# Weighing four units of attention at once in every second slot, with six buffers of exponentials

## The chip, the cores and the metric

The kernel runs on one core of a Trainium2 chip. A core has a matrix engine (TensorE; PE in the profile, its weight loads PEld), a vector engine (VectorE, DVE), an activation engine (ScalarE, ACT), GpSimd (POOL) and SyncE (SP), which issues most transfers. Each engine runs its own list of instructions in order; semaphores hold them together. The metric is the device time of one execution in microseconds (us). The kernel before takes 1525.11 us, the median of three runs (1524.86 to 1526.01).

## The reference, cut to what matters

The input is a batch of eight images of 32 x 32 positions (1024 tokens) with 256 channels, in float32. Three layers follow each other, each added to its input:

```python
x = x + conv_ref(gn(x), ...)   # linear attention: 8 heads of 32; out = q @ (k^T v) / n
t = to_tokens(x)               # 8 batches x 1024 tokens x 256
t = t + attn_ref(ln(t), ...)   # softmax attention:
#   scores = q @ k^T / sqrt(32);  attn = softmax(scores);  sa = attn @ v;  out = sa @ w_agg + b_agg
t = t + ffn_ref(ln(t), ...)    # 8 experts: gates by 8 Sinkhorn iterations, each expert takes its
#   128 best tokens per batch, multiplies them by its 256 x 256 matrix and puts them back
```

The softmax attention is the largest part: per batch and head 1024 x 1024 scores, their exponentials, and the product of the exponentials with the values.

## The kernel before, in words

**Units, slots, steps.** The softmax attention of one batch is 64 units (2 groups of four heads, 4 blocks of 256 queries, 8 tiles of 128 keys). A unit has three parts. `scores(u)`, on the matrix engine (L918), is four matmuls, one for each head, over the full width of 128 columns, into one of two PSUM tiles `score_ps[u % 2]`. `exponential(u)`, on the activation engine (L1209), is one instruction of 128x1024 elements into `probs[:, u % PROBS, :]`. `weigh(u)`, on the matrix engine again (L940), multiplies the exponentials by the values: each head needs only 32 columns, so four matmuls stand in the four column quarters of the array (`tile_position=(0, 32 r)`) and run beside each other. Float32 matmuls are two instructions each, so that a unit is four L918 instructions and eight L940 ones in the trace. The row sums of the exponentials are added up by the vector engine for the first six key tiles of a block (`add_up`, L1607) and by the matrix engine for the last two (L937), in the same narrow form; `total` (L950) ends a block of eight units.

Two units make a slot, so a batch has 32 slots and the eight batches 256. Beside the units the slots carry steps: the linear attention and the projections of the next batch (its "front": `xT`, `gmean`, `gvar`, `xn`, `qk0`, `v0`, `qT`, `dots`, `lin`, `zT`, `proj`, `v`, `norms`) and the end of the batch before (its "store": `agg`, `z2T`, `gate`). In batches 5 to 7 (counted from 0) the routing of the experts is merged in. `order()` lists the steps with entries `("rest", n)`, which leave n slots free of them; `spread()` deals the list to slots by the weights in `WORK`, and `Slot.halves` cuts each slot's steps in two.

**The order inside a slot k** is, on the matrix engine:

```python
for u in (2 * k + 2, 2 * k + 3): scores(u)
for st in first: step(*st)
weigh(2 * k)
weigh(2 * k + 1)
for st in second: step(*st)
```

and on the activation engine `exponential(2k+2)`, first half of the steps, `exponential(2k+3)`, second half.

**What waits for what.** `scores(u)` waits for `exponential(u - 2)`, which frees its PSUM tile. `exponential(u)` waits for `scores(u)`, and for `weigh(u - PROBS)` and for the vector engine's sum of unit `u - PROBS`, which free its buffer. `weigh(u)` waits for `exponential(u)`; `total` waits for the last sum of its block. The steps of the matrix engine share three PSUM banks in turn (`shared_ps`); each is filled by a step, read by ACT or DVE, and can then be filled again. Some steps also need a result at once: `proj` (L962) needs the copies `chan` that ACT makes (L1137) of the transposes `zT` (L957); `gmean` (L962 on `small`) needs the statistics that DVE makes of `xT`; `xn` on DVE (L1417) needs a reciprocal root that POOL works out in 14 small instructions (L361 to L366) after `gvar`.

**The tail.** Experts' tokens are gathered and put back by `indirect_dma_start` on POOL (`pick`, L1309, and `put`, L1319), in batch 7 and behind it. The descriptors of these transfers are written by POOL into a scratch region of the on-chip memory, whose size is an argument of the program's constructor.

## Time and profile before

| | us |
|---|---|
| median of three runs | 1525.11 |
| the profiled execution's own time | 1524.4 |
| its span in the profile | 1520.8 |
| matrix engine busy | 1343.5 (88%) |
| vector engine busy | 1017.4 (67%) |
| activation engine busy | 864.4 (57%) |
| GpSimd busy | 549.0 (36%) |

The time outside the span is 3.6 us. In the trace the attention of batch 0 runs from 110 to 267 us, batches 1 to 4 take 153 us each up to 880, batch 5 goes to 1040, batch 6 to 1206, batch 7 to about 1370, and the rest is the tail. A matmul's start in a row is recorded and its end is modelled, so the text works with differences of starts. In a row, `x16` says how many instructions were merged, and the brackets at its end give the idle time before it and what ended it.

### The profile page before, as it was taken

The numbers are of one execution on the slowest core, as the hardware profiler recorded it, in microseconds if no ns is written. First come the engines' busy times: TensorE is split into PE (matmuls) and PEld (weight loads), VectorE is DVE, ScalarE is ACT, GpSimd is POOL, SyncE is SP. The second block draws the span as 40 slices with busy tenths as digits, with TensorE's granted clock in tenths as the row PEclk, the third lists the DMA queues.
The fourth block names the chain that finished last, engine by engine and source line by source line (L and its number), as shares of the span: only waits on it lengthen the run. The fifth ranks groups of instructions, "written<-read, shape, count | busy, mean of one in ns | idle before, by whom it ended". The sixth has DMA issues, their size and how long they took to land.

```text
span 1520.8 us, 29096 instructions
## 1 busy us (share of the span) xinstructions
PE 1343.5 (88%) x10849; PEld 917.5 (60%) x10849; DVE 1017.4 (67%) x2077; ACT 864.4 (57%) x1260; POOL 549.0 (36%) x1126
## 2 busy tenths in 40 slices
PE   4688989999999999999999999899998988887633
PEld 3555566667666766676667666657665656555522
DVE  3416766758575857585758575977789757588781
ACT  1346657667666766676667666566656664342100
POOL 1341620345034503450345034412353046643443
PEclk7999999999999999999999999999999998997666
DMA  2043003600360036003600360027000573433422
GB/s 76 3 127 81 2 29 84 167 15 29 84 167 15 29 84 167 15 29 84 167 15 29 84 167 15 1 72 195 27 1 1 133 216 104 119 118 105 123 73 81
DMA packets 66787, 119.15 MB, mean 78 GB/s; under 512 B 10705, under 2 KB 46546, under 8 KB 66642
## 3 DMA queue, kind: packets, MB, share of 16 engines
q1 hardware_dynamic: 56640, 90.47, 22.1%
q0 software_dynamic: 8960, 26.75, 5.9%
q8 instruction: 89, 1.46, 0.4%
q14 instruction: 56, 0.46, 0.1%
q10 hardware_dynamic: 1042, 0.01, 0.0%
HBM read 29.11 MB, written 33.55 MB: 41 GB/s over the span
## 4 chain that ended last, share of the span: by engine, by line
PE 57%; DVE 24%; issue 7%; ACT 4%; POOL 4%; another core or an unknown queue 2%; DMA 0%; POOLq 0%; DVEq 0%; ACTq 0%
PE shared L962 27%; PE scores L918 11%; PE acc L940 10%; DVE prob_sum L1607 6%; PE acc L937 4%; DVE acc_sb L1581 3%; ACT probs L1209 3%; PE shared L957 2%; DVE bn L1340 2%; PE acc L950 2%; DVE best_i L1513 1%; DVE work L1515 1%; DVE best L1511 1%; DVE bn_x L1393 1%
## 5 line engine op out<-in xcount | busy, mean ns | idle before, releaser
L1209 ACT ACTIVATE probs<-scores 128x1024 f32<-128x1024 f32 x512 | 516.7, 1023 | 180.7 <-PE scores L918 91.7
L918 PE MATMUL scores<-query_stack,key_stack 96*128 96x256 f32 x2048 | 343.3, 308 | 13.9 <-ACT probs L1209 11.3
L1607 DVE TENSOR_TENSOR prob_sum<-prob_sum,probs 128x512 f32<-128x512 f32 x512 | 333.0, 712 | 0.0
L918 PEld LDWEIGHTS scores<-query_stack,key_stack 96*128 96x128 f32 x2048 | 275.3, 190 | 83.8 <-issue 42.3
L940 PE MATMUL acc<-probs,v_all 128*32 128x256 f32 x4096 | 293.2, 390 | 7.0 <-issue 5.3
L1242 POOL TENSOR_TENSOR attn_T<-acc_sb 128x256 f32<-128x256 f32 x56 | 45.7, 817 | 447.0 <-DVE acc_sb L1581 442.9
L962 PE MATMUL shared<-w_sb,chan 128*128 128x512 f32 (+1 forms) x512 | 188.0, 503 | 5.0 <-DVE chan L1417 5.0
L940 PEld LDWEIGHTS acc<-probs,v_all 128*32 128x32 f32 x4096 | 115.8, 110 | 107.3 <-issue 42.4
L962 PEld LDWEIGHTS shared<-w_sb,chan 128*128 128x128 f32 x512 | 92.1, 193 | 67.8 <-issue 63.7
L962 PE MATMUL shared<-chan,w1T 128*128 128x512 f32 x256 | 120.9, 606 | 1.6 <-ACT chan L1137 1.6
L1581 DVE RECIPROCAL acc_sb<-acc_sb 128x256 f32<-128x256 f32 x64 | 111.4, 1741 | 0.0
L1466 DVE TENSOR_TENSOR lo<-shared,hi 128x512 fp32r<-128x512 f32 x64 | 43.4, 684 | 99.6 <-ACT hi L1162 99.6
L1607 DVE TENSOR_TENSOR prob_sum<-probs 128x512 f32<-128x512 f32 x128 | 98.8, 812 | 11.4 <-PE acc L950 8.9
L1432 DVE TENSOR_REDUCE ss<-v_all 128x16 f32<-128x512 f32 x64 | 43.8, 684 | 91.0 <-ACT v_all L1151 90.9
L1144 ACT ACTIVATE lo<-shared 128x512 f32<-128x512 f32 x64 | 38.2, 597 | 107.6 <-PE shared L962 107.6
L937 PE MATMUL acc<-probs,ones 128*32 128x256 f32 x1024 | 84.8, 395 | 1.4 <-issue 1.1
L962 PEld LDWEIGHTS shared<-chan,w1T 128*128 128x128 f32 x256 | 46.7, 192 | 49.8 <-issue 49.2
L1192 ACT ACTIVATE hi<-shared 128x512 f32<-128x512 f32 (+1 forms) x31 | 16.0, 515 | 102.7 <-PE shared L1079 54.2
L1471 DVE TENSOR_REDUCE norm_max<-shared 128x1 f32<-128x512 f32 x64 | 43.6, 682 | 41.3 <-PE shared L962 41.3
L1162 ACT ACTIVATE hi<-shared 128x512 fp32r<-128x512 f32 x64 | 37.5, 594 | 49.4 <-PE shared L962 49.4
L957 PE MATMUL shared<-ident,rows 128*128 128x128 f32 x252 | 43.6, 286 | 22.2 <-ACT rows L1116 14.2
L962 PE MATMUL shared<-waggT,attn_T 128*128 128x256 f32 x244 | 61.4, 387 | 1.7 <-ACT hi L1192 1.7
(216 smaller groups left out, 2069.0 us busy)
## 6 DMA issues: line engine op xcount, KB each, us to landing
query_stack<-hi SPq DMA_DIRECT2D x120, 128.0 KB, 2.5
key_stack<-hi SPq DMA_DIRECT2D x120, 128.0 KB, 2.5
x_sb<-in_x_dram SPq DMA_DIRECT2D x8, 1024.0 KB, 5.3
out_dram<-resid SPq DMA_DIRECT2D x16, 512.0 KB
tokens_scratch<-resid SPq DMA_DIRECT2D x16, 512.0 KB
tokens_scratch<-rows SPq DMA_DIRECT2D x16, 512.0 KB, 4.7
key_stack<-lo SPq DMA_DIRECT2D x60, 128.0 KB, 2.5
query_stack<-lo SPq DMA_DIRECT2D x60, 128.0 KB, 2.5
```

Of the source, the lines that this page charges most:

```text
L918: last = pe.matmul(score_ps[u % 2][:, QB * r:QB * (r + 1)], key_stack[stack, HG * g + r, P * kt:P * (kt + 1)], query_stack[stack, HG * g + ...
L937: pe.matmul(acc[DH * r:DH * (r + 1), QB:2 * QB], ones[:, 0:DH], p[:, QB * r:QB * (r + 1)], start=False, stop=False, skip_group_check=True, ...
L940: last = pe.matmul(acc[DH * r:DH * (r + 1), 0:QB], v_all[:, g, kt, DH * r:DH * (r + 1)], p[:, QB * r:QB * (r + 1)], start=kt == 0, stop=kt ...
L957: last = pe.transpose(ps[:, P * j:P * (j + 1)], m, ident[:, :])
L962: last = pe.matmul(out, stationary, moving, start=j == 0, stop=j == len(pairs) - 1)
L1209: act.activation(probs[:, u % PROBS, :], score_ps[u % 2][:, :], ACT.Exp, scale=DH ** -0.5) \
L1242: pool.tensor_tensor(attn_T[:, g, QB * qb:QB * (qb + 1)], acc_sb[:, 0:QB], acc_sb[:, QB:2 * QB], ALU.mult).then_inc(s["attn_ready"], 1)
L1432: dve.tensor_reduce(ss[:, t, :], squares[:, t % 2, :].rearrange("p (h d) -> p h d", d=DH), AX.X, ALU.add).then_inc(s["squares_summed"], 1)
L1466: read(dve.tensor_tensor(lo[:, j, part].bitcast(F32R), ps[:, :], hi[:, j, part], ALU.subtract), seg, *st)
L1471: read(dve.tensor_reduce(norm_max[:, seg.front, j, h:h + 1], ps[:, :], AX.X, ALU.max), seg, *st)
L1581: dve.reciprocal(acc_sb[:, QB:2 * QB], acc_sb[:, QB:2 * QB]).then_inc(s["recip_ready"], 1)
L1607: dve.tensor_tensor(total[:, part], probs[:, (u - 1) % PROBS, part] if kt == 1 else total[:, part], probs[:, u % PROBS, part], ALU.add).th ...
```

## The change

Three constants and the list of steps change. In slots with an odd number the matrix engine now weighs four units in a row, in slots with an even number none; `scores` and `exponential` stay where they were, two in each slot.
```diff
-PROBS = 4
+PROBS = 6
@@ order()
-    steps = [("rest", 0.5), ("xT", 1, 0), ("xT", 0, 1), ("agg", 0), ("agg", 1), ("agg", 2), ("agg", 3),
+    steps = [("xT", 1, 0), ("rest", 0.5), ("xT", 0, 1), ("agg", 0), ("agg", 1), ("agg", 2), ("agg", 3),
...
@@ the matrix engine's loop over slots
-                if k is not None:
-                    weigh(2 * k)
-                    weigh(2 * k + 1)
+                if k is not None and k % 2:
+                    for u in range(2 * k - 2, 2 * k + 2):
+                        weigh(u)
                     if k % BLOCK_PAIRS == BLOCK_PAIRS - 1:
                         total(k // BLOCK_PAIRS)
@@ kernel()
-    nc = _bacc.Bacc("TRN2", target_bir_lowering=False, num_devices=1)
+    nc = _bacc.Bacc("TRN2", target_bir_lowering=False, num_devices=1,
+                     dynamic_dma_scratch_size=8192)
```

Three places show how it moves instructions. In the order of a program a float32 matmul counts once, so a unit is x4 of `acc<-probs,v_all`.

The first is the matrix engine in slots 20 to 23 of batch 1, where few steps lie. Before:

```order
L918 MATMUL scores<-query_stack,key_stack 128x256 x8
L940 MATMUL acc<-probs,v_all 32x256 x8
L918 MATMUL scores<-query_stack,key_stack 128x256 x8
L940 MATMUL acc<-probs,v_all 32x256 x8
L918 MATMUL scores<-query_stack,key_stack 128x256 x8
L962 MATMUL shared<-hi 128x128 x8
L940 MATMUL acc<-probs,v_all 32x256 x8
L918 MATMUL scores<-query_stack,key_stack 128x256 x8
```

Now:

```order
L918 MATMUL scores<-query_stack,key_stack 128x256 x16
L957 MATMUL shared<-ident,lo 128x128 x4
L940 MATMUL acc<-probs,v_all 32x256 x16
L918 MATMUL scores<-query_stack,key_stack 128x256 x8
L962 MATMUL shared<-hi 128x128 x6
L918 MATMUL scores<-query_stack,key_stack 128x256 x8
L962 MATMUL shared<-hi 128x128 x2
```

The scores of slots 20 and 21 (x16) stand next to each other with nothing between them, and one group of four units follows where two groups of two were; the transposes `ident,lo` (step `qT`) came from slot 19, and one of the `lin` steps (`hi`) went to slot 23.

The second is the vector engine in slots 1 to 4 of batch 0: `small` are the statistics of the steps `x_stats`, `gmean` and `gvar` (L1412), `chan` is `xn`, `prob_sum` the sums of the units. Before:

```order
L1400 COPY small<-mv_x 128x2
L1403 COPY small<-shared 128x2
L1406 TENSOR_TENSOR small<-small 128x2
L1407 TENSOR_TENSOR small<-small 128x2
L1408 TENSOR_TENSOR small<-small,mv_x 128x2
L1607 TENSOR_TENSOR prob_sum<-prob_sum,probs 128x512 x4
L1471 TENSOR_REDUCE norm_max<-shared 128x1
L1412 TENSOR_SCALAR small<-shared 128x2
L1417 TENSOR_SCALAR chan<-chan,small 128x512 x2
L1607 TENSOR_TENSOR prob_sum<-prob_sum,probs 128x512 x4
```

Now:

```order
L1400 COPY small<-mv_x 128x2
L1607 TENSOR_TENSOR prob_sum<-prob_sum,probs 128x512 x4
L1471 TENSOR_REDUCE norm_max<-shared 128x1
L1403 COPY small<-shared 128x2
L1406 TENSOR_TENSOR small<-small 128x2
L1407 TENSOR_TENSOR small<-small 128x2
L1408 TENSOR_TENSOR small<-small,mv_x 128x2
L1412 TENSOR_SCALAR small<-shared 128x2
L1607 TENSOR_TENSOR prob_sum<-prob_sum,probs 128x512 x4
L1417 TENSOR_SCALAR chan<-chan,small 128x512 x2
```

The last sums of the first block (the second x4) stood behind `chan` and now stand ahead of it; the product `gmean` is read one slot later.

The third is the matrix engine in slots 24 and 25 of batch 1. Before:

```order
L957 MATMUL shared<-ident,rows 128x128 x8
L940 MATMUL acc<-probs,v_all 32x256 x8
L962 MATMUL shared<-chan,w1T 128x512 x4
L918 MATMUL scores<-query_stack,key_stack 128x256 x8
L962 MATMUL shared<-chan,w1T 128x512 x2
```

Now:

```order
L957 MATMUL shared<-ident,rows 128x128 x8
L962 MATMUL shared<-chan,w1T 128x512 x4
L918 MATMUL scores<-query_stack,key_stack 128x256 x8
L962 MATMUL shared<-chan,w1T 128x512 x2
L962 MATMUL shared<-norm_sq,head_ones 128x512
```

The group of narrow matmuls that stood between the transposes `zT` (L957) and the first `proj` (`chan,w1T`) is gone from there.

## Rows read from the trace of the kernel before

**Rows 1.** The page: busy us, share of the span and instructions of each engine.

```profile
PE 1343.5 (88%) x10849; PEld 917.5 (60%) x10849; DVE 1017.4 (67%) x2077; ACT 864.4 (57%) x1260; POOL 549.0 (36%) x1126
```

**Rows 2.** Windows, batches 3, 5, 6: length, busy PE, PEld, DVE, ACT, POOL; clock; DMA.

```profile
573.85:727.00 153.15, 151.03 (x1309) 102.87 (x1306) 103.90 (x194) 105.63 (x154) 52.66 (x125) 1.00 0.28 74
...
880.00:1040.20 160.20, 153.57 (x1297) 102.42 (x1296) 124.05 (x243) 103.25 (x150) 52.69 (x125) 1.00 0.26 69
1040.20:1206.20 166.00, 155.60 (x1310) 105.42 (x1306) 133.34 (x281) 105.72 (x153) 58.81 (x125) 0.98 0.23 61
```

**Rows 3.** Timeline, batch 2, slots 20 to 22: start, duration, engine, instructions.

```profile
517.12 1.21 PE L918 MATMUL scores<-query_stack,key_stack 96*128 96x256 f32 x8
518.26 1.07 PE L940 MATMUL acc<-probs,v_all 128*32 128x256 f32 x16
519.26 1.36 PE L918 MATMUL scores<-query_stack,key_stack 96*128 96x256 f32 x8
...
521.56 1.21 PE L918 MATMUL scores<-query_stack,key_stack 96*128 96x256 f32 x8
...
522.33 1.94 ACT L1209 ACTIVATE probs<-scores 128x1024 f32<-128x1024 f32 x2 [0.35 <-PE scores L918]
522.61 1.95 PE L962 MATMUL shared<-hi 128*128 128x128 f32 x16
```

**Rows 4.** Timeline in windows of 0.15 us: single matmuls about slot 23, batch 2.

```profile
525.16 0.40 PE L940 MATMUL acc<-probs,v_all 128*32 128x256 f32 x4
525.49 0.39 PE L918 MATMUL scores<-query_stack,key_stack 96*128 96x256 f32 x1
...
525.71 0.52 PE L918 MATMUL scores<-query_stack,key_stack 96*128 96x256 f32 x3
526.31 0.40 PE L918 MATMUL scores<-query_stack,key_stack 96*128 96x256 f32 x2
526.64 0.42 PE L937 MATMUL acc<-probs,ones 128*32 128x256 f32 x4
```

**Rows 5.** Timeline, batch 2, slot 19: one long group of narrow matmuls.

```profile
515.28 0.61 PE L940 MATMUL acc<-probs,v_all 128*32 128x256 f32 x8
515.72 0.61 PE L937 MATMUL acc<-probs,ones 128*32 128x256 f32 x8
```

**Rows 6.** Lines, 410 to 570 us: ACT's steps, mean ns of one.

```profile
L1116 ACT ACTIVATE rows<-resid,ln_b,ln_r 128x256 f32<-128x256 f32 x8 | 4.6, 592 | 2.5 <-POOLq L1256 2.5
L1157 ACT ACTIVATE hi<-shared,gb 128x512 f32<-128x512 f32 x4 | 3.1, 772 | 0.0
L1132 ACT ACTIVATE hi<-shared 128x256 f32<-128x256 f32 x8 | 3.0, 389 | 0.0
```

**Rows 7.** Timeline, batch 2, slots 14, 15, 24: what ACT gives to the matrix engine.

```profile
494.92 1.03 ACT L1209 ACTIVATE probs<-scores 128x1024 f32<-128x1024 f32 x1 [1.08 <-DVE prob_sum L1607]
...
497.64 0.74 PE L918 MATMUL scores<-query_stack,key_stack 96*128 96x256 f32 x4 [0.50 <-ACT probs L1209]
...
530.78 1.10 ACT L1137 ACTIVATE chan<-shared 128x512 f32<-128x512 f32 x2
531.11 1.07 PE L940 MATMUL acc<-probs,v_all 128*32 128x256 f32 x16
```

**Rows 8.** Timeline, batch 3, slot 2: the wait of `gmean`.

```profile
586.09 1.03 PE L962 MATMUL shared<-waggT,attn_T 128*128 128x256 f32 x4
588.42 0.35 PE L962 MATMUL shared<-small,gn_mean 128*128 128x2 f32 x2 [1.29 <-DVE small L1400]
```

**Rows 9.** Timeline, batch 0, slots 2 and 3: DVE and PE.

```profile
124.75 1.00 DVE L1417 TENSOR_SCALAR chan<-chan,small 128x512 f32<-128x512 f32 x2 [3.67 <-POOLq L1268]
...
128.22 0.64 PE L950 MATMUL acc<-prob_sum,ones 128*32 128x256 f32 x8 [3.67 <-DVE prob_sum L1607]
```

**Rows 10.** Timeline of POOL, batch 7: the last gathers of a burst of nine.

```profile
1253.86 0.94 POOL L1309 DMA_INDIRECT hi<-tokens_scratch,slot_token  x1 [0.30 <-issue]
1255.11 0.94 POOL L1309 DMA_INDIRECT hi<-tokens_scratch,slot_token  x1 [0.30 <-issue]
```

More of the change, by code:

```diff
@@ new lines, in order @@
+             ("store_rows", 0), ("rest", 1), ("store_rows", 1), ("gmean",), ("agg", 7), ("store_rows", 2),
+             ("gvar",), ("store_stats", 1), ("xn", 0), ("z2T", 0), ("store_rows", 3), ("z2T", 1), ("z2T", 2),
+             ("z2T", 3), ("gate", 0), ("rest", 2), ("qk0", 0), ("gate", 1), ("store_rows", 4), ("qk0", 1),
+             ("gate", 2), ("store_rows", 5), ("xn", 1), ("store_rows", 6), ("z2T", 4), ("rest", 1), ("gate", 3),
[3 rows of a table added]
+             ("head_scale", 0), ("resid", 3), ("resid", 4), ("v0", 6), ("head_scale", 1), ("qk0", 7), ("resid", 5),
@@ L109, in order @@
+             ("zT", 1, 0), ("rest", 0.25), ("zT", 0, 0), ("proj", 0, 0), ("front_rows", 4), ("square", 0, 0),
+             ("proj", 2, 0), ("proj", 1, 0), ("norms", 0, 0), ("square", 1, 0), ("front_rows", 5),
+             ("front_rows", 6), ("front_rows", 7), ("norms", 1, 0), ("square", 2, 0), ("proj", 3, 0), ("zT", 0, 1),
              ("zT", 1, 1), ("norms", 2, 0), ("proj", 0, 1), ("square", 3, 0), ("proj", 1, 1), ("rest", 0.5),
```

21 lines of the change are left out of this document (5 added, 16 removed), and 3 rows, old and new, of the table steps.

## The prediction

> **What bounds the kernel now.** I read the page's engine shares, then windows of one batch each, then the timeline of one steady batch, then single matmuls. The matrix engine is busy 88% of the span and the others 67% or less [rows 1]. In batch 3, which stands for batches 1 to 4, it is busy 151.0 of 153.2 us at clock 1.00, with DVE at 104 and ACT at 106 [rows 2]: there the matrix engine sets the time. In batches 5 and 6 DVE has 124 and 133 us of work, and the batches take 160 and 166: there the sinkhorn and top-k steps on DVE hold the matrix engine back in the middle of the batch. Batch 7 and the tail hang partly on the gathers.
>
> **What a group of narrow matmuls costs beyond its matmuls.** Inside a long group a unit takes 0.44 us [rows 5], two quartets of 0.22. Around a group [rows 4]: the last quartet starts at 525.16 and the first scores at 525.49, 0.33 and not 0.22; the second scores follow at 525.71, 0.22 later, where the next five take 0.12 each (525.71 to 526.31); and the last two steps, 526.31 to 526.64, are 0.33, of which 0.12 is one cadence and 0.21 the way into the next group. So a group costs 0.11 + 0.10 + 0.09 = 0.30; its first quartet is some 0.02 longer. The group of two units alone agrees (518.26 to 519.26 [rows 3]): 1.00 where two units inside a long group are 0.87. The 0.10 may be less behind transposes; without it the price is 0.22. I take 0.31.
>
> The Trainium skill (TensorEngine Tiling, section Tiling Modes, Key Properties) says that changing the tiling mode drains the engine and gives no price. By it the merged group would save the same, so the sum doesn't change.
>
> **Term 1, fewer groups.** Eight batches of 32 slots are 256 groups; 128 remain. 128 x 0.31 = 40 us, or 5.0 us per batch (28 to 41 us over all by the two ends). In the middle of batches 5 and 6 and in the second half of batch 7, about 20 of the 128, the matrix engine waits for others anyway, so some 6 of the 40 don't show.
>
> **Term 2, the cover that goes.** The weighing also hid the exponentials. From the start of a slot's scores to the first exponential 0.77 us pass (521.56 to 522.33), and two exponentials take 1.94 [rows 3], so the second ends 2.71 us into the slot. The second scores of the next slot need it. In an even slot with steps of length c the matrix engine gets there after 1.05 (two scores, 521.56 to 522.61) + c + 0.47. The wait is therefore 1.25 - c (with some 0.05 for the signal), plus the time A of those steps that ACT does between its two exponentials. Before, 1.09 us of weighing and its entry stood in between, and the rule gives 0.16 for an empty slot; the row shows 0.15 (scores of 1.36 at 519.26 against 1.21 at 517.12 [rows 3]), so I trust it. With ACT's steps of 0.59, 0.77 and 0.39 [rows 6], the even slots of a steady batch in the new order are:
>
> - slots 16, 20 and 30 have no step on the matrix engine: 3 x 1.25 = 3.75;
> - slot 14 has two `qT` transposes (c 0.88, A 0.77): 1.14;
> - slot 4 has c 1.28 (three or four `z2T`, a `gate`), and ACT does z2T, store_rows, z2T between the exponentials, A 1.37: 1.34;
> - slot 2 has one `agg` (c 0.86): 0.4; slots 0, 6 to 12, 18, 22 to 28 have 1.3 or more of c against it: 0.
>
> That is 6.6. In slots 24 and 26 another cover goes: `proj` needs the copies of `zT`, which ACT finished at 530.78 + 1.10 = 531.88, while the group that began at 531.11 hid it [rows 7]. Without the group `proj` starts 0.8 late, twice: 1.6. Term 2 is 8.2 us per steady batch. In an odd slot four units take at least 1.74 + 0.31 us, so nothing waits there.
>
> **Term 3, waits that go.** `gmean` waits 1.46 us in every steady batch (586.09 to 588.42, less the 0.86 of `agg` [rows 8]). It moves behind the next slot's scores, and its statistics are then ready. In slot 15 the scores wait because the exponential before them waited 1.08 for DVE's sum to free its buffer [rows 7]; six buffers lift that wait, about 0.8. Five waits of 0.16 as above are replaced by term 2's: 0.8. Together 3.1. The `dots` and `norms` waits, 0.6 together, I leave.
>
> **The other batches.** *Batches 1 to 4:* -5.0 + 8.2 - 3.1 = +0.1 each, that is 0. *Batch 0:* `gmean` waits for its statistics and `total` waits for the last sums, which stand behind `xn`, which waits 3.67 for POOL [rows 9]. Now those sums stand ahead of `xn`, and `gmean` is a slot later. 3.7 goes there, `gmean`'s wait (taken as the 1.46 of [rows 8]) and 5.0 of groups go too, and new waits of about 1 in slot 2 and 3 in slots 24 to 30 come: -6.2. What comes in the middle falls beside older waits. *Batch 5:* -4 for groups, -2.7 for old waits as in a steady batch, +4 for even slots (sinkhorn products fill some, DVE's waits swallow others): -2.7. *Batch 6:* -3.5, -1.5, +3.5: -1.5. *Batch 7:* in slots 2 to 10 new waits of 3.5 against some 2.5 of old ones for DVE's sums of the kind in [rows 7] (an estimate), groups -3 where they show: -2. *The tail and the front:* same instructions, 0.
>
> **Buffers and scratch.** The two buffers cost no instruction. The gathers follow each other at 1.25 us in a burst of nine with 0.30 between them [rows 10]: POOL isn't short of descriptor space there, and I take 0 for half the scratch. The bounds are 0 and one landing time per burst, of which I have no row; by the nearest rows, one step of 1.25 us for each of the eight bursts or so, 10 us.
>
> The Trainium skill (SBUF - State Buffer, section SBUF size: 192, 224, or 256?) gives 16 KiB per partition to the ring of descriptors that GpSimd fills. By it the change leaves 8 KiB, and this is the one rule that speaks against it. No row here shows a ring that is full.
>
> **Sum.** 4 x 0 - 6.2 - 2.7 - 1.5 - 2 = -12.4, with the 0.1 left over per steady batch -12, say -13 us since the 0.6 of `dots` and `norms` can only shrink. The profiled execution took 1524.4 us (span 1520.8 and 3.6 around it), 0.7 under the median, so 1511 us. In totals: the groups give 35, old waits give some 26, new waits take some 48. The result is a small difference of large terms, and this sets the range.
>
> **The clock.** New waits are at most 1.3 us each. Batches 1 to 4 keep 1.00 with waits of 1.46 in them, batch 5 too, and batch 6 shows 0.98 [rows 2]. I take no loss; a batch at 0.98 would cost 3 us. The Trainium skill (TensorE: Matmul & The Clock Gate, Why this matters for your kernels) warns of idle gaps between bursts of matmuls; by the rows the new ones are too short for it, and the sum stays.
>
> **Rivals.**
>
> *A, the cover isn't needed (15%).* Half of the new waits don't appear, because ACT runs ahead with six buffers or because dependent steps were late anyway: 1511 - 24 = 1487. For it: in batches 5 to 7 others' waits can swallow them. Against it: `scores(u)` needs `exponential(u - 2)` whatever the number of `probs` buffers, and the check on an empty slot above was exact.
>
> *B, slower: steps without the pause (14%).* Before, every slot had 1 us in which ACT and DVE emptied the three shared banks and made operands. In the 10 even slots with steps, that pause is gone. If each of them loses 0.4 us on banks and operands beyond what I have counted, 7 batches x 10 x 0.4 = 28 us: 1539. It decides from 0.19 us per such slot, where it eats my 13 us. For it: the copies of `zT` show one such case at 0.8. Against it: ACT and DVE have 48 us free per batch, and a bank is refilled only after two other steps.
>
> *C, the scratch stalls POOL (3%).* 10 us, all in batch 7 and the tail: 1521.
>
> *D, nothing comes of it (12%).* New waits are 13 us larger than I count, for instance since ACT's steps push both exponentials in more slots: 1524.
>
> **How the numbers follow.** My forecast has 56%. Its own range is 1500 to 1520, from 0.22 to 0.32 per group (12 us) and from 20% on either side of 48 us. The range reaches from rival A's time to just over D's, 1488 to 1528. Within 0.2% (3 us, about what a measurement of this kernel tells from none) is D and a little of B, C and the forecast: 0.13. Faster: A's 15, C's 2, nearly all of the forecast's 56 and the space between: 0.73. Slower: 0.14.
>
> **What the new profile would show.** Groups of four units 1.87 us long; scores in slots 17, 21, 31 with a wait of 1.2 on ACT `probs`, slot 15 with 1.1; steady batches of 153 us again, batch 0 near 150; `gmean` without a wait; `total` of batch 0's first block without its 3.67; ACT's waits for `prob_sum` nearly gone; POOL's gathers still 1.25 us apart in bursts. I am wrong if steady batches are under 150 (term 2 too large) or over 156 (rival B, seen as waits for `chan`, `hi` or DVE results in even slots).

## The result, and the profile after

The changed kernel takes 1531.76 us (median of 5 runs, 1530.11 to 1532.86) where the kernel before takes 1525.11: ratio 1.0042, 95% interval 1.0028 to 1.0057. It is 0.4% slower. I had forecast 1511 us, in a range of 1488 to 1528, and gave slower a chance of 0.14. The prediction was wrong.

The page of the kernel after: engine shares, then four groups of instructions (busy us, mean ns | idle us before them, releaser).

```profile
PE 1321.5 (87%) x10849; PEld 933.2 (61%) x10849; DVE 1016.9 (67%) x2077; ACT 860.4 (56%) x1260; POOL 560.2 (37%) x1126
...
L1209 ACT ACTIVATE probs<-scores 128x1024 f32<-128x1024 f32 x512 | 511.9, 1024 | 121.5 <-PE scores L918 102.8
L918 PE MATMUL scores<-query_stack,key_stack 96*128 96x256 f32 x2048 | 344.8, 308 | 34.6 <-ACT probs L1209 32.4
...
L1607 DVE TENSOR_TENSOR prob_sum<-prob_sum,probs 128x512 f32<-128x512 f32 x512 | 332.8, 710 | 0.0
...
L962 PE MATMUL shared<-chan,w1T 128*128 128x512 f32 x256 | 122.4, 612 | 10.1 <-ACT chan L1137 8.7
```

The instruction counts are those of [rows 1], and the matrix engine is busy 22 us less: half of the groups, and the pauses around them, are gone. But the scores now wait 34.6 us, 32.4 of it for ACT's exponentials, and `proj` waits 8.7 us for ACT's copies. DVE's sums wait for nothing. The same two lines on the page of the kernel before:

```profile
L918 PE MATMUL scores<-query_stack,key_stack 96*128 96x256 f32 x2048 | 343.3, 308 | 13.9 <-ACT probs L1209 11.3
L962 PE MATMUL shared<-chan,w1T 128*128 128x512 f32 x256 | 120.9, 606 | 1.6 <-ACT chan L1137 1.6
```

Windows of the kernel after, in the columns of [rows 2]: batch 0, then 3, 5, 6, then 7.

```profile
110.20:271.00 160.80, 143.17 (x1224) 96.24 (x1224) 105.75 (x169) 102.67 (x144) 45.17 (x92) 0.96 0.21 50
...
574.70:726.50 151.80, 145.99 (x1300) 103.06 (x1296) 103.80 (x194) 104.58 (x152) 54.00 (x125) 1.00 0.28 74
878.40:1041.50 163.10, 153.04 (x1316) 107.45 (x1312) 122.94 (x243) 104.82 (x152) 52.83 (x125) 0.99 0.26 69
1041.50:1208.50 167.00, 153.07 (x1310) 107.47 (x1306) 132.50 (x281) 105.14 (x153) 63.27 (x125) 0.97 0.23 61
...
1208.60:1376.80 168.20, 141.49 (x1197) 102.80 (x1193) 109.51 (x245) 79.26 (x109) 82.38 (x105) 0.92 0.45 136
```

The window of batch 3 in [rows 2] reaches 1.1 us into batch 4. Cut to the batch, the kernel before shows:

```profile
573.85:725.91 152.06, 149.94 (x1300) 101.78 (x1296) 103.90 (x194) 104.73 (x152) 52.66 (x125) 1.00 0.28 74
```

In batch 3 the matrix engine is busy some 4 us less than before and idle 3.7 us more, and the batch is nearly as long. What the groups gave went into waits.

A batch is measured here from the start of its first own scores to the next batch's (batch 7's to the start of its slot 30). In us (the differences are of unrounded times, the last column is the sum of my terms in the prediction):

| batch | before | after | difference | forecast |
|---|---|---|---|---|
| 0 | 159.4 | 160.9 | +1.5 | -6.2 |
| 1 | 152.7 | 151.8 | -0.8 | 0 |
| 2 to 4, each | 152.1 | 151.8 | -0.2 | 0 |
| 5 | 162.3 | 163.1 | +0.8 | -2.7 |
| 6 | 166.0 | 167.0 | +1.0 | -1.5 |
| 7 | 160.2 | 168.2 | +8.0 | -2 |
| from there to the end | 154.4 | 149.3 | -5.0 | 0 |

The steady batches came out as forecast in all, and several pairs of slots did by themselves: 30-31 are 0.86 longer (worked out: 1.25 less 0.16 less 0.31 is 0.78), 2-3 are 1.19 shorter (0.4 - 1.46 - 0.31 is -1.37), 24-25 are 0.59 longer (0.8 - 0.31 is 0.49), and four pairs with enough work are 0.31 to 0.34 shorter (0-1, 12-13, 22-23, 28-29). In the other pairs the moved steps mix with the grouping (8-9 are 1.4 shorter, 20-21 are 1.3 longer). The new waits stand where they were expected. Timelines of the kernel after, batch 3: the scores of slot 21 behind an empty slot 20, and `proj` behind `zT` in slot 24.

```profile
667.85 1.22 PE L918 MATMUL scores<-query_stack,key_stack 96*128 96x256 f32 x8
...
668.63 2.88 ACT L1209 ACTIVATE probs<-scores 128x1024 f32<-128x1024 f32 x3
669.70 0.74 PE L918 MATMUL scores<-query_stack,key_stack 96*128 96x256 f32 x4 [0.64 <-ACT probs L1209]
670.62 0.74 PE L918 MATMUL scores<-query_stack,key_stack 96*128 96x256 f32 x4 [0.17 <-ACT probs L1209]
```

```profile
682.34 1.08 ACT L1137 ACTIVATE chan<-shared 128x512 f32<-128x512 f32 x2
683.52 3.67 PE L962 MATMUL shared<-chan,w1T 128*128 128x512 f32 x8 [0.79 <-ACT chan L1137]
```

Eight matmuls of scores take 1.21 us without a wait [rows 3]. Here the two units of slot 21 start 1.85 and 2.77 us behind the start of slot 20. ACT goes from one exponential to the next, and the matrix engine is bound to it.

The old waits went too. Timeline of the kernel after, batch 3, slots 2 and 3: `gmean` waited 1.29 in [rows 8] and waits 0.18.

```profile
588.37 0.74 PE L918 MATMUL scores<-query_stack,key_stack 96*128 96x256 f32 x4 [0.18 <-ACT probs L1209]
589.29 0.35 PE L962 MATMUL shared<-small,gn_mean 128*128 128x2 f32 x2 [0.18 <-DVE small L1400]
```

The miss lies in batches 0, 5, 6 and 7, by 7.7, 3.5, 2.5 and 10 us; the tail gives 5.0 of it back, for which I had no term. The tail's gain is no gain of the grouping: it takes 149.6 us in `e3` below too, which is the kernel before but for the scratch. And batch 6 is not a firm number: the changed kernel's takes 163.9 to 167.0 us from one trace to another. One place in batch 0 stands out. Its slots 22 and 23 took 12.0 us and take 18.0. Timeline and windows of the kernel after, about slot 22 of batch 0.

```profile
216.15 1.08 PE L957 MATMUL shared<-ident,rows 128*128 128x128 f32 x4 [3.15 <-ACT rows L1116]
216.88 2.06 PE L918 MATMUL scores<-query_stack,key_stack 96*128 96x256 f32 x8
218.74 1.06 PE L957 MATMUL shared<-ident,rows 128*128 128x128 f32 x4
220.53 3.75 PE L962 MATMUL shared<-chan,w1T 128*128 128x512 f32 x4 [0.73 <-issue]
224.21 1.65 PE L940 MATMUL acc<-probs,v_all 128*32 128x256 f32 x16
```

```profile
216.00:220.00 4.00, 3.65 (x16) 3.27 (x16) 2.64 (x8) 1.80 (x4) 2.99 (x9) 0.50 0.82 262
220.00:224.50 4.50, 3.97 (x8) 1.38 (x12) 0.00 (x0) 0.61 (x2) 1.52 (x8) 0.50 0.00 0
```

`zT` waits 3.15 us for ACT's rows, and the matmuls behind it run at a granted clock of 0.50, the lower level of 1.2 GHz: scores of 2.06 where 1.21 is usual, `proj` of 3.75 where it takes about 2. The stretch lasts 10 us.

The kernel before had lost its clock in batch 0 too, three times for 3.4 us, and once behind waits far shorter than these. Timeline and window of the kernel before, batch 0, slots 18 and 19:

```profile
203.04 0.74 PE L918 MATMUL scores<-query_stack,key_stack 96*128 96x256 f32 x4 [1.06 <-ACT probs L1209]
204.62 1.22 PE L918 MATMUL scores<-query_stack,key_stack 96*128 96x256 f32 x4 [0.84 <-ACT probs L1209]
```

```profile
204.00:208.00 4.00, 3.38 (x28) 2.03 (x32) 2.18 (x8) 2.50 (x3) 1.22 (x6) 0.57 0.00 0
```

### The profile page after: what moved, and what is told of

It is laid out like the page before. It is cut to its first block, busy times and chain, and to the rows that moved or that the text cites. A ratio compares the mean times of both kernels' runs of the same rounds, so it can differ in the third digit from the quotient of the medians.

```text
span 1526.0 us, 29094 instructions
## 1 busy us (share of the span) xinstructions
PE 1321.5 (87%) x10849; PEld 933.2 (61%) x10849; DVE 1016.9 (67%) x2077; ACT 860.4 (56%) x1260; POOL 560.2 (37%) x1126
## 3 DMA queue, kind: packets, MB, share of 16 engines
q8 instruction: 89, 1.46, 0.4%
## 4 chain that ended last, share of the span: by engine, by line
PE 57%; DVE 19%; issue 9%; ACT 7%; POOL 6%; another core or an unknown queue 1%; ACTq 0%; POOLq 0%; DVEq 0%
PE shared L962 29%; PE acc L940 10%; PE scores L918 10%; DVE prob_sum L1607 5%; ACT probs L1209 3%; PE acc L937 3%; PE shared L957 2%; PE acc L950 2%; DVE acc_sb L1581 1%; DVE best_i L1513 1%; DVE work L1515 1%; DVE best L1511 1%; DVE bn L1340 1%; ACT chan L1137 1%
## 5 line engine op out<-in xcount | busy, mean ns | idle before, releaser
L1209 ACT ACTIVATE probs<-scores 128x1024 f32<-128x1024 f32 x512 | 511.9, 1024 | 121.5 <-PE scores L918 102.8
L918 PE MATMUL scores<-query_stack,key_stack 96*128 96x256 f32 x2048 | 344.8, 308 | 34.6 <-ACT probs L1209 32.4
L940 PE MATMUL acc<-probs,v_all 128*32 128x256 f32 x4096 | 279.0, 388 | 1.8 <-issue 1.7
L962 PE MATMUL shared<-w_sb,chan 128*128 128x512 f32 (+1 forms) x512 | 184.9, 499 | 6.1 <-DVE chan L1417 5.8
L940 PEld LDWEIGHTS acc<-probs,v_all 128*32 128x32 f32 x4096 | 122.1, 111 | 101.9 <-issue 30.9
L1607 DVE TENSOR_TENSOR prob_sum<-probs 128x512 f32<-128x512 f32 x128 | 92.1, 760 | 0.0
L1199 ACT ACTIVATE acc_sb<-acc 128x512 f32<-128x512 f32 x64 | 38.0, 593 | 66.3 <-PE acc L950 53.9
L1253 POOL TENSOR_SCALAR ln_v<-mv 128x4 f32<-128x4 f32 x30 | 11.0, 367 | 155.6 <-DVE mv L1358 154.2
```

The source lines that it names most:

```text
L918: last = pe.matmul(score_ps[u % 2][:, QB * r:QB * (r + 1)], key_stack[stack, HG * g + r, P * kt:P * (kt + 1)], query_stack[stack, HG * g + ...
L940: last = pe.matmul(acc[DH * r:DH * (r + 1), 0:QB], v_all[:, g, kt, DH * r:DH * (r + 1)], p[:, QB * r:QB * (r + 1)], start=kt == 0, stop=kt ...
L962: last = pe.matmul(out, stationary, moving, start=j == 0, stop=j == len(pairs) - 1)
L1209: act.activation(probs[:, u % PROBS, :], score_ps[u % 2][:, :], ACT.Exp, scale=DH ** -0.5) \
L1607: dve.tensor_tensor(total[:, part], probs[:, (u - 1) % PROBS, part] if kt == 1 else total[:, part], probs[:, u % PROBS, part], ALU.add).th ...
```

## The experiments

The ratios are to the kernel before on the same chip, with their 95% intervals. The kernel before itself took 1521.4, 1500.1, 1521.6, 1499.4 and 1521.5 us in the five comparisons: there are two kinds of chip here. Times are compared within a comparison, and pieces of a trace across comparisons only for batches 0 to 6. These show no difference between the kinds, but one trace differs from another of the same kernel by up to 0.8 us in batch 0, 2 us in batches 3 and 4 and 3 us in batch 6.

### Taking the change apart

`e1_old_steps` keeps the grouping, the buffers and the scratch, and takes the list of steps back.

```diff
-    steps = [("xT", 1, 0), ("rest", 0.5), ("xT", 0, 1), ...
+    steps = [("rest", 0.5), ("xT", 1, 0), ("xT", 0, 1), ...   # as before, whole list
```

> The change with the list of steps of the kernel before: four units weighed in every odd slot, six buffers, half the scratch, steps as they were. Theory G (grouping saves 0.31 us a group and takes the cover from even slots; the loss against forecast is in batch 0 slots 22-23, where the new list puts a transpose that waits for ACT rows and the clock halves, and in batch 7): batch 0 gets back some 5 of its 6 us there, steady batches lose the moved gmean (1.5 us each) and get more waits in slots 2 and 4: 1530 to 1540 in all. Rival S (the new steps are to blame): under 1520.

Measured: 1563.33 us, ratio 1.0281 (1.0250 to 1.0311), 23 us over the range expected. Slots 22 and 23 of batch 0 came down to 10.7 us without a half clock, as expected. But batches 1 to 4 take 157.5 to 160.8 us and batches 5 and 6 169.0 and 169.8, and in each of batches 2 to 4 the granted clock is at 0.50 for 3.4 to 6.8 us: on the old list the grouping costs far more in a steady batch than the moved `gmean`.

`e2_pairs_new_steps` keeps all but the grouping.

```diff
-                if k is not None and k % 2:
-                    for u in range(2 * k - 2, 2 * k + 2):
-                        weigh(u)
+                if k is not None:
+                    weigh(2 * k)
+                    weigh(2 * k + 1)
```

> The change without the grouping: two units weighed in every slot as before, with the new list of steps, six buffers and half the scratch. Theory G: the groups cost again 0.31 us each but the cover is back; gmean's wait (1.46 us, batches 1 to 6), DVE's sums (0.8) and batch 0's 3.7 us are gone: 1505 to 1515, batch 7 near 160 us. Rival S (new steps) or rival R (half the scratch): 1530 or more. If six buffers and the new list bring nothing: 1525.

Measured: 1512.32 us, ratio 0.9946 (0.9927 to 0.9965). Batches 154.5, four times 151.8, 161.9, 166.4, 156.6.

`e3_scratch` is the kernel before with the smaller scratch alone.

```diff
-    nc = _bacc.Bacc("TRN2", target_bir_lowering=False, num_devices=1)
+    nc = _bacc.Bacc("TRN2", target_bir_lowering=False, num_devices=1,
+                     dynamic_dma_scratch_size=8192)
```

> The kernel before with half the scratch for dynamic DMAs and nothing else. Theory G: no difference, 1525 within 1. Rival R (half the scratch stalls POOL's gathers and puts in batch 7 and the tail): 1530 to 1535, batch 7 near 168 us instead of 160.

Measured: 1522.63 us, ratio 1.0003 (0.9988 to 1.0018).

`e4_six_buffers` adds the two buffers to it.

```diff
-PROBS = 4
+PROBS = 6
```

> The kernel before with six buffers of exponentials and half the scratch, pairs weighed in every slot, old steps. Theory G: the exponentials no longer wait for DVE's sums: slot 15 wins 0.8 us in batches 1 to 6, a bit more in the DVE-bound middles of 5 and 6 and in batch 7: 1515 to 1521. Rival R: 1530.

Measured: 1514.54 us, ratio 0.9960 (0.9946 to 0.9975); batch 0 is 5.4 us shorter than before, batch 7 2.0. In batch 0 slots 18-19 give 3.0 of it (the kernel before has a half clock there, this one not), 22-23 1.8 and 30-31 0.5; slots 0 to 5 are as long as before.

What follows: half the scratch costs nothing. Six buffers give 0.4%, mostly in batch 0. The new list with two units per slot adds little (0.9946 against 0.9960, intervals that overlap). The grouping then loses: from 0.9960 to 1.0281 on the old list, from 0.9946 to about 1.004 on the new one. The list was needed for the grouping, and even with it the grouping costs 0.9% (`e9` and `e10` below).

### Is the price of a group real?

`e7_split_groups` starts from the two-unit kernel and splits the group in eight slots of batches 1 to 6.

```diff
+                split = k is not None and 32 <= k < 224 and k % 32 in (1, 8, 9, 10, 11, 12, 28, 29)
+                if split:
+                    weigh(2 * k)
                 for st in first:
                     step(*st)
                 if k is not None:
-                    weigh(2 * k)
+                    if not split:
+                        weigh(2 * k)
                     weigh(2 * k + 1)
```

> The kernel with new steps, six buffers and two units in every slot, in which eight slots (1, 8, 9, 10, 11, 12, 28, 29) of batches 1 to 6 weigh their first unit ahead of the slot's first steps and the second behind them: the same matmuls, 48 more groups. Theory (each group costs 0.31 us by itself, whatever it hides): +14.9 us, 1527; each of these slots 0.31 longer. Rival (a group costs nothing, and what merging gains is waits): within 2 us of 1512.

Measured: 1516.58 us, ratio 1.0128 (1.0109 to 1.0147), against 0.9946 without the split. In batches 1 to 4 slots 1, 9, 10, 11 and 29 are each 0.29 to 0.34 longer than in `e2`, which is the price. Slots 8, 12 and 28 are 0.4 to 0.7 longer, slots that were not split (4, 15, 16) up to 0.2, and each batch by 3.8 to 4.0 in all where 2.5 was forecast. Over batches 1 to 6 it is 22.6 us and not 14.9. So a group does cost 0.3 us by itself, and the rival, that it costs nothing, is out; but moving a unit cost half as much again in other ways, and I have not traced those.

### Where the grouping loses

`e8_pairs_slot22` takes one group of the 128 back, the one of slots 22 and 23 of batch 0.

```diff
+            def joined(k):
+                return k != 23
...
-                if k is not None and k % 2:
-                    for u in range(2 * k - 2, 2 * k + 2):
-                        weigh(u)
+                if k is not None:
+                    if k % 2 and joined(k):
+                        for u in range(2 * k - 2, 2 * k + 2):
+                            weigh(u)
+                    elif k % 2 or not joined(k + 1):
+                        weigh(2 * k)
+                        weigh(2 * k + 1)
```

> The changed kernel with one group of 128 taken back: slots 22 and 23 of batch 0 weigh two units each. Theory (the lost 1.2 us of cover in slot 22 leaves a wait of 3 us for ACT's rows there, the clock halves behind it for 10 us, and this is 5 of batch 0's lost microseconds): slots 22 and 23 fall from 18.0 to about 13.2 us, no half clock there, total about 1527. Rival (the wait only moves, or the clock halves anyway): slots 22 and 23 stay above 16.5, total 1530 to 1532.

Measured: 1493.97 us, ratio 0.9960 (0.9946 to 0.9973), on a chip of the faster kind, where the changed kernel itself shows 0.9987 (below). Slots 22 and 23 take 13.17 us; every other pair of batch 0 but 14-15 (+0.34) is within 0.04 of the changed kernel. Timeline and window of this kernel at the same place.

```profile
214.36 1.07 PE L940 MATMUL acc<-probs,v_all 128*32 128x256 f32 x16
217.58 0.63 PE L957 MATMUL shared<-ident,rows 128*128 128x128 f32 x4 [2.15 <-ACT rows L1123]
217.97 1.21 PE L918 MATMUL scores<-query_stack,key_stack 96*128 96x256 f32 x8
...
220.35 1.96 PE L962 MATMUL shared<-chan,w1T 128*128 128x512 f32 x4 [0.74 <-issue]
```

```profile
216.00:220.00 4.00, 2.03 (x16) 1.82 (x16) 3.97 (x12) 3.19 (x6) 1.97 (x4) 1.00 0.52 164
```

The weighing stands in the wait for ACT's rows: 2.15 us are left of 3.15, the clock stays at 1.00, `proj` takes 1.96 and not 3.75. Between these two traces one group returned is worth 4.86 us. `zT` starts 4.8 us into slot 22 in both, so about 1 us of it is the weighing that no longer stands in the wait, and the rest is the clock.

One trace doesn't make a rule of the clock. Slots 22 and 23 of batch 0 in every trace with the new list (us; the third column is the time at 0.50 in them):

| kernels | wait of `zT` | at 0.50 | slots 22-23 |
|---|---|---|---|
| grouped there: the changed kernel's first trace, `e6`, `e13`, `e14`, `e16`, `e17`, `e18` | 3.15 | 10.2 | 18.0 to 18.3 |
| grouped there: `e9`, `e11`, `e15` | 3.15 | 6.8 | 16.9 |
| two units each: `e2`, `e7`, `e8`, `e10` | 2.14 or 2.15 | 0 | 13.2 |
| two units each: `e12` | 2.15 | 3.4 | 14.7 |
| two units each: `e5` | 2.15 | 6.8 | 16.0 |

Behind 3.15 us the clock fell every time, behind 2.15 in two traces of six. Timeline and window of `e5`, the same place with the same wait as in `e8`:

```profile
219.22 0.63 PE L958 MATMUL shared<-ident,rows 128*128 128x128 f32 x4 [2.15 <-ACT rows L1125]
...
222.57 3.75 PE L963 MATMUL shared<-chan,w1T 128*128 128x512 f32 x4 [0.73 <-issue]
```

```profile
221.00:225.00 4.00, 3.27 (x7) 1.61 (x7) 0.72 (x2) 0.99 (x2) 2.93 (x14) 0.50 0.48 166
```

So the group returned is worth 4.86 us in this pair of traces and 3.8 on the average of the ten and the six. What else decides in this place is open.

`e6_pairs_in_batch7` takes batch 7's grouping back (`return k // 32 != 7` in the same edit).

> The changed kernel with the grouping taken back in batch 7 alone (two units in every slot there). Theory (batch 7's 8 us are the grouping there: the expert steps and DVE's sums had been hidden by the weighing of every slot): batch 7 falls from 168 to about 157, total about 1520. Rival (batch 7 is late because of what comes before it, or because the new steps or the scratch delay its gathers): batch 7 stays over 165, total about 1530.

Measured: 1499.32 us, ratio 1.0001 (0.9984 to 1.0018), batch 7 135.5 us. I had expected about 157; the chip was of the faster kind, and alone this told nothing. The next comparison put the kernels side by side on a chip of the slower kind.

> The changed kernel once more, beside the next three on one chip, since the kernel before took 1525, 1521 and 1500 us on the three chips so far and the difference lay in batch 7. Theory (the grouping costs 11.6 us in batch 7 only where the gathers are late, and 2.1 where they aren't): ratio to the kernel before 1.004 if that kernel takes over 1515 us here, about 0.999 if it takes 1500. Rival (the ratio belongs to the kernel): 1.004 on every chip.

Measured (the changed kernel): 1528.20 us, ratio 1.0033 (1.0019 to 1.0048). Its batches 3 and 4 take 153.5 us each and not 151.8. Timeline and window of this trace, batch 3, slots 16 and 17:

```profile
651.29 1.21 PE L918 MATMUL scores<-query_stack,key_stack 96*128 96x256 f32 x8
653.21 0.74 PE L918 MATMUL scores<-query_stack,key_stack 96*128 96x256 f32 x4 [0.71 <-ACT probs L1209]
654.13 0.95 PE L918 MATMUL scores<-query_stack,key_stack 96*128 96x256 f32 x4 [0.18 <-ACT probs L1209]
```

```profile
654.00:656.00 2.00, 1.87 (x10) 1.87 (x11) 2.00 (x2) 1.04 (x3) 2.00 (x3) 0.62 0.03 8
```

The clock falls for 3.4 us behind waits of 0.71 and 0.18, which the grouping brought, with another of 0.78 one slot earlier. That costs 1.6 us. The first trace of the changed kernel has the same waits there and stays at 1.00; of the eleven traces with this grouping in batches 3 and 4, four lose the clock (`e9`, `e11`, `e15`, `e17`), each time in both batches.

> New steps, six buffers, half the scratch, two units in every slot. Theory: ratio to the kernel before 0.995 as on the other chip; the changed kernel minus this one: +6.4 us in batch 0, 0 in batches 1 to 4, +1.8 in 5 and 6 together, +2 to +12 in batch 7 by the gathers. Rival: the difference between the two is spread or less than 5 us in all.

Measured (the kernel of `e2`): 1513.78 us, ratio 0.9943 (0.9920 to 0.9965).

> The changed kernel with two units per slot in batch 7 alone. Theory: all batches as in the changed kernel, batch 7 shorter by 2 us if the gathers are early on this chip and by 8 to 12 if they are late; the total by the same. Rival (what batch 7 takes is set before it): same time as the changed kernel within 1.5 us.

Measured (the kernel of `e6`): 1520.60 us, ratio 0.9986 (0.9974 to 0.9999); its batch 7 is 9.4 us shorter than the changed kernel's.

So on one chip the grouping costs 16.9 us of span (1524.8 against 1507.9): +7.2 in batch 0, +1.6 in batches 1 to 6 together, +10.6 in batch 7, and the rest is -2.6. Batches 0 and 7 are as expected; batches 1 to 4 are not (+2.9 where 0 was expected, nearly all in batches 3 and 4, with the clock), nor are 5 and 6 together (-1.3 and not +1.8). In batch 0 slots 22-23 lose 3.7 and slots 14-15 3.1, both with 6.8 us at half clock where the two-unit kernel has none. In slots 14-15 it falls behind waits of 0.73, 0.63 and 1.97 us close together, while the two-unit kernel keeps it behind a single one of 2.25. In batch 7 slots 6 to 13 lose 5.6 of it (3.4 in slots 12-13, with 12.6 us at half clock against 6.8) and slots 18-19 another 5.0. Timeline of the changed kernel (`e9_after_again`), slot 19 of batch 7, inside its group of four units.

```profile
1304.41 0.38 PE L937 MATMUL acc<-probs,ones 128*32 128x256 f32 x1 [0.85 <-issue]
...
1304.43 1.09 PE L940 MATMUL acc<-probs,v_all 128*32 128x256 f32 x4
...
1305.86 1.09 PE L940 MATMUL acc<-probs,v_all 128*32 128x256 f32 x4 [0.34 <-issue]
...
1307.29 0.63 PE L950 MATMUL acc<-prob_sum,ones 128*32 128x256 f32 x4 [0.34 <-issue]
...
1308.70 0.61 PE L950 MATMUL acc<-prob_sum,ones 128*32 128x256 f32 x3 [0.78 <-issue]
```

Quartets that start 0.22 apart elsewhere [rows 5] start 1.42 apart, with no semaphore behind it. This group takes 11.4 us where its matmuls need about 3.2. The two-unit kernel shows the same rhythm once, in a shorter stretch (`e10_pairs_again`, same slot):

```profile
1290.74 0.62 PE L940 MATMUL acc<-probs,v_all 128*32 128x256 f32 x4 [0.36 <-issue]
1292.15 0.41 PE L940 MATMUL acc<-probs,v_all 128*32 128x256 f32 x2 [0.78 <-issue]
```

On the faster kind of chip no narrow matmul inside a group of batch 7 starts more than 0.5 us after the one before it, and the grouping costs 2.1 us there (137.6 in `e8` against 135.5 in `e6`); on another chip of that kind it costs nothing (136.3 in `e13` against 137.5 in `e14`, below). Nor is this rhythm all of what the slower kind loses: `e11` on it takes 157.1 us for batch 7 with a single narrow matmul that late, in slot 25. Its slots 12-13 take 21.6 us where `e6` has 15.1 (13.7 us at half clock against 3.4), and its slots 18-19 16.1 against 9.8.

The last kernels ask whether the DMA traffic of the gathering phase makes the instructions late. `e15_small_puts` and `e16_small_puts_pairs7` write 8 of 128 rows per scatter and leave the others out.

```diff
-                                                bass.IndirectOffsetOnAxis(ap=slot_token[:, e, b:b + 1], axis=0),
-                                                picked[d % PICKED][:, j, 0:C], None) \
+                                                bass.IndirectOffsetOnAxis(ap=slot_token[0:8, e, b:b + 1], axis=0),
+                                                picked[d % PICKED][0:8, j, 0:C], None) \
```

> The changed kernel, as the reference of the next three on this chip. If the kernel before takes about 1520 us here: batch 7 takes 166 to 168, with matmuls of the long group in slot 19 starting four every 1.42 us. If it takes about 1500: batch 7 takes 138 and there are no such steps.

Measured (the changed kernel): 1498.00 us, ratio 0.9987 (0.9973 to 1.0001), batch 7 136.3.

> Two units per slot in batch 7 alone, as the second reference: 8 to 11 us under the changed kernel on a chip where batch 7 is long, 2 us on one where it is short.

Measured: 1498.39 us, ratio 0.9992 (0.9979 to 1.0004), batch 7 137.5, longer by 1.2 and not shorter by 2.

> The changed kernel, whose experts' results are written back for 8 of 128 rows per scatter; the other rows stay out, so this write traffic of the gathering phase is a sixteenth, and every instruction is there. Theory (the matrix engine's instructions come late in batch 7 because the DMA engines are loaded by gathers and scatters): the steps of 1.42 us in slot 19 go, batch 7 falls by more than 8 us. Rival (the steps have to do with the length of the group or with the engine itself): they stay, and batch 7 falls by less than 3 us.

Measured: 1496.37 us, ratio 0.9977 (0.9965 to 0.9988), batch 7 134.5.

> The same with two units per slot in batch 7. Theory (the grouping costs batch 7 so much only through the late instructions): with the small scatters the difference between this and the grouped one is about 2 us in batch 7, as on the chip with the short batch 7. Rival (it is dependent steps that lose their cover): the difference stays 8 us or more.

Measured: 1498.71 us, ratio 0.9993 (0.9975 to 1.0012), batch 7 133.4. The chip was of the faster kind, where the slow rhythm is absent: nothing is told apart. The repetition fell on the slower kind.

> The changed kernel as reference of the next. Theory: ratio 1.003 to 1.004 and batch 7 of 166 to 168 us where the kernel before takes about 1520 us, 0.999 and 138 us where it takes about 1500.

Measured (the changed kernel): 1531.35 us, ratio 1.0062 (1.0039 to 1.0084), batch 7 166.7.

> The changed kernel with scatters of 8 of 128 rows, the others staying out. It tells something only on a chip where batch 7 is long. Theory (write traffic delays the matrix engine's instructions): batch 7 falls by more than 8 us and the steps of 1.42 us in slot 19 go. Rival (it doesn't): less than 3 us, and they stay.

Measured: 1526.04 us, ratio 1.0031 (1.0017 to 1.0046), batch 7 164.5. Slots 18-19 lose 4.1 us and the rhythm is gone from slot 19, but 22-23 and 26-27 are 3.6 longer: the batch is 2.2 shorter, not 8. The rival's bound holds, though not its second half. The whole kernel is 5.3 us shorter (1526.04 against 1531.35); in the two traces 3.3 us of the difference lie in batches 3 and 4, where the clock didn't fall this time. So writing a sixteenth of the rows doesn't take batch 7's length away. The gathers stayed as they were, and no kernel here tests them; the cause stays open. The 16 KB packets of the instruction queue are not it either as far as the trace shows: in `e9` one starts at 1291.4 and the next at 1314.1, none in the slow stretch between.

### A version that beats both

`e5_joined_good` joins four units only where the even slot has work for the matrix engine; the numbers are the odd slots of joined pairs, one set per batch.

```diff
+JOINED = ({9, 11, 17, 21, 29},) + 6 * ({1, 7, 9, 11, 13, 19, 23, 25, 27, 29},) + (set(),)
...
+            def joined(k):
+                batch, second_slot = divmod(k, 32)
+                return second_slot in JOINED[batch]
```

> As the changed kernel (new steps, six buffers, half the scratch), but four units are weighed together only in slot pairs with enough matrix-engine work in their even slot: in batches 1 to 6 pairs 0-1, 6-7, 8-9, 10-11, 12-13, 18-19, 22-23, 24-25, 26-27, 28-29, in batch 0 pairs 8-9, 10-11, 16-17, 20-21, 28-29, in batch 7 none; 65 of 128. Elsewhere two units in every slot. Theory (the price of a group is real, and the loss is the cover in slots without work and beside dependent steps): the sum of the differences of these pairs between the ungrouped and the grouped traces with new steps, about -3.9 in each of batches 1 to 4, -3 and -2 in batches 5 and 6, -1.5 in batch 0, is -22 against 1512, so about 1490. Steady batches 147.9. Rival (what a joined pair gains is lost in the pair behind it, because its operands are then not ready): steady batches 151 and about 1510.

Measured: 1488.88 us, ratio 0.9925 (0.9908 to 0.9942). The total is near the 1490 expected only because of the chip: by the ratio it is 1510 where the kernel before takes 1521.4 (an estimate), the rival's figure. Steady batches 149.3, between the theory's 147.9 and the rival's 151: a joined pair beside one that isn't keeps only part of its gain (6-7 gives 0.22 and not 0.37, 18-19 nothing). Batch 0 took 159.2, 4.8 more than with two units everywhere. Nearly all of it stands in slots 14-15 and 22-23 (2.9 each), which are not joined: the clock fell there for 6.8 us each. Joining other slots was enough to lose it.

`e12_joined_better` keeps only `{17, 21, 29}` in batch 0.

> The kernel that joins four units only in slot pairs with work in the even slot, now in batch 0 for slots 16-17, 20-21 and 28-29 alone. Theory: batch 0 falls from 159.2 to about 153.5 (154.5 with two units everywhere, less 3 groups of 0.33), steady batches 149.3 again, total about 1.3% under the kernel before. Rival (batch 0's time goes by the clock and not by these groups): batch 0 stays at 157 or more, about 0.8% under.

Measured: 1504.04 us where the kernel before takes 1521.63, ratio 0.9874 (0.9855 to 0.9894). It is the fastest against the kernel before. Against two units in every slot on the same chip (`e10`, 1513.78) the joined pairs give 0.6%; the rest of the 1.3% is the buffers' and the list's. Batch 0 takes 155.2 where 153.5 was expected, with 3.4 us at half clock in slots 22-23. Windows of this kernel, batches 2 and 3.

```profile
415.10:564.40 149.30, 147.01 (x1300) 102.37 (x1296) 103.75 (x194) 104.42 (x152) 53.94 (x125) 1.00 0.28 75
564.40:713.70 149.30, 147.00 (x1300) 102.40 (x1296) 103.94 (x194) 104.62 (x152) 53.34 (x125) 1.00 0.28 75
```

## Why the prediction was wrong

**Term 1, fewer groups: right.** Against two units in every slot (`e2`), merging gives 0.27 to 0.37 in seven pairs of a steady batch where nothing new waits. Splitting costs 0.29 to 0.34 in five of eight slots, though the others lost more. The busy time of the matrix engine fell by some 4 us in batch 3 and not by 5.0; as the ends of matmuls are modelled, I trust the starts more.

**Term 2, the cover in steady batches: right for the scores, in part by luck in the sum.** The waits stand in the slots named (pair 30-31: 0.78 forecast, 0.86 measured), and batches 1 to 4 moved by -0.8 and three times -0.2 against a forecast of 0. But `proj`'s wait was put down to the wrong thing. With the new list and two units per slot it waits even longer (`e2`, batch 3, slot 24):

```profile
677.00 1.96 PE L962 MATMUL shared<-chan,w1T 128*128 128x512 f32 x4 [1.15 <-ACT chan L1137]
```

The list moved `proj` ahead of the weighing; the grouping only left it at 0.79. By my terms the grouping should have cost a steady batch 2.4 us (5.0 less of groups, 8.2 of lost cover, 0.8 of old waits), and the list and the buffers should have given 2.3. Measured through `e2`, the grouping costs 0.1 and the list and the buffers give 0.3. The two misses cancel, and that is luck.

**Term 3, waits that go: right in kind.** `gmean` and DVE's sums no longer hold anything up, in batch 0 too, whose slots 0 to 5 are 4.2 us shorter. Neither needs the grouping, and the two causes can be told apart. `gmean`'s wait went with the list: slots 2-3 of a steady batch take 9.6 us before and in `e4`, which has six buffers and the old list, and 7.9 in `e2`. DVE's sums are the buffers' part: slots 14-15 take 7.3 us before and 6.6 in `e4`. In `e4` slots 0 to 5 of batch 0 are as long as before, so the gain there is not the buffers' (`e2` has 2.5 of the 4.2 us, and loses its clock for 6.8 us in slots 2-3, where the changed kernel's first trace does not). But the new list costs other slots of a steady batch what it gives these: `e2` is only 0.3 us shorter than the kernel before.

**The other batches: the step that failed.** "What comes in the middle falls beside older waits" was written of batch 0, and "DVE's waits swallow others" was the same thought for batch 5. A group that goes from an even slot was counted at nothing where something waited there already. In slot 22 the reverse is true: the weighing had filled 1 us of the wait, and without it the matrix engine stands idle for that time and does the work later. By my count the grouping was worth -1 in batch 0 (-5.0 for groups, 4 for new waits), and +7.2 was measured against two units per slot on one chip. Slots 22-23 and 14-15, the middle that I had put at nothing, are 6.8 of it.

**The clock: put at nothing, and it took part of the loss in batches 0 and 7.** "New waits are at most 1.3 us each" and "I take no loss" looked at new waits by themselves. In slot 22 the new one was laid on an old one (2.40 us in the kernel before, 2.15 with the new list and two units), and with 3.15 the clock was lost in all ten traces, for 6.8 or 10.2 us. The Trainium skill (TensorE: Matmul & The Clock Gate, Why this matters for your kernels) warns of idle gaps between bursts of matmuls. I set the rule aside because I weighed it against each new wait and not against the sum of new and old; the ten traces agree with it. It would not have found the other losses: 1.6 us each in batches 3 and 4 of four traces, behind waits of 0.78 us and less. I could have known of these. "Too short for it" went by the rows of batches 1 to 6, while batch 0 of the kernel before lost its clock behind waits of 1.06 and 0.84 us. In batch 0 the time at half clock is 17.1 us in `e9` and 6.8 in `e10`; at half rate 10 us more of it are worth up to 5 us of the 7.2, an estimate.

**Batches 5 and 6: -2.7 and -1.5 forecast, +0.8 and +1.0 measured.** Against two units per slot they move by +0.3 and -1.6 on one chip and by +1.3 and +0.7 between `e2` and the changed kernel's first trace. This is as much as traces of one kernel differ among themselves, so no more can be said than that the groups I counted there (-4 and -3.5) hardly show. I did not follow which waits take them.

**Batch 7: -2 forecast, +8.0 measured.** Slots 6 to 13 lose 5.6 us against two units per slot, 3.4 of it in slots 12-13 with the clock at half for longer; which waits lost their cover there I have not followed. In slots 18-19 the instructions come late inside a group that is now twice as long, and why they come late stays open. Taking the grouping back in batch 7 alone returns 9.4 us on such a chip (`e11`), so the loss is the grouping's even where its cause is open. That a batch could be slow in a way that depends on the chip was nowhere in my range: the changed kernel is at 1.003 to 1.006 of the kernel before on one kind and at 0.9987 on the other.

**Buffers and scratch: right.** 0 for half the scratch, measured 1.0003; rival C is out. Rival B had the right side. Its mechanism, a pause lost in slots with steps, comes nearest to slot 22, but it was priced at 0.4 us in every such slot, and without the clock: a steady batch shows nothing of it, and a single pair of slots in batch 0 3.7 to 4.9 us.

Against its own kin the change is worth less than its parts: on one chip 1513.8 without the grouping (`e10`), 1528.2 with it (`e9`). The gain from groups was paid back in waits, in steady batches one for one and in batches 0 and 7 with interest.

## What to carry to other kernels

Work that pauses the dependent chain is cover. Before merging it, list per slot what waits there already, and add the new wait to the old, and to its neighbours, before asking what the clock does. Then merge only where the slot has other independent work: on one chip that selection took 1504.0 us, two units in every slot 1513.8, merging everywhere 1528.2 and the kernel before 1521.6. And hold a forecast against a version that leaves the one change out: a total that comes true can be two misses.

## What the runs showed of the hardware

- A group of 32-column matmuls between matmuls of 128 columns costs about 0.3 us by itself: 0.27 to 0.37 by merging (seven pairs of slots, changed kernel against `e2`), 0.29 to 0.34 by splitting (five slots, `e7` against `e2`).
- In one place the granted clock of the matrix engine fell to 0.50 behind a wait of 3.15 us in ten traces of ten, for 6.8 or 10.2 us, and behind one of 2.15 in two of six (`e5`, `e12`).
- In another it fell for 3.4 us behind waits of 0.78, 0.71 and 0.18 us within some 7 us, in four traces of eleven, and cost 1.6 us (11.47 and 9.85 us for the same two slots in `e9` and in the changed kernel's first trace).
- The same kernel takes 1500 us on some chips and 1521 on others, and nearly all of it is the last batch: 135.5 against 157.1 us for the same instructions (`e6` and `e11`). On the slower kind the matrix engine there starts four narrow matmuls every 1.42 us for stretches of up to 9 us, with no releaser in the trace (`e9`). Cutting the scatters' rows to a sixteenth moved these stretches and shortened the batch by 2.2 us of 166.7 (`e18`, `e17`).
- Half the scratch for dynamic DMAs made no difference (1.0003, 0.9988 to 1.0018) with bursts of nine gathers.
